# The sine product of the exchanged key halves on GpSimd instead of VectorE

## The reference, cut to what matters

```
x_attn = _L0_xattn_ref(_layernorm(x), ctx_4096, ctx_4096, mask, wq, wk, wv, wo, 0)

k = (key @ wk).reshape(bs, sk, N_KV_HEADS, 1, D_K)
rotate_half(x) = concatenate([-x2, x1])          # x1, x2: the halves of the 128
k = k * cos[None, None] + rotate_half(k) * sin[None, None]
raw = einsum('bhqd,bhkd->bhqk', q, k) / sqrt(D_K)
attn = softmax(raw + mask)
out = einsum('bhqk,bhkd->bhqd', attn, v)
```

## Time and profile before

| what | value |
|---|---|
| runs | 1937.64, 1943.05, 1941.91 us; median 1941.91 |
| the profiled execution | 1944.6 us, its span 1942.7 us |
| mean granted clock of TensorE | 0.984 |
| busy: TensorE, VectorE, ScalarE, GpSimd | 96%, 80%, 52%, 61% of the span |

### The profile page before, as it was taken

The page is one execution under the profiler, slowest core; times in us unless marked ns, Lnnn a source line. Parts: engine busy times, 40 slices in busy tenths (PEclk is TensorE's granted clock), DMA queues, the critical chain, the costliest instruction groups (busy, mean ns, idle before and its releaser), DMA issues. The chain is left out here.

```text
span 1942.7 us, 36348 instructions
## 1 busy us (share of the span) xinstructions
PE 1863.1 (96%) x12454; PEld 1706.5 (88%) x12454; DVE 1552.9 (80%) x2598; ACT 1019.1 (52%) x1882; POOL 1194.0 (61%) x990
## 2 busy tenths in 40 slices
PE   7989999999999999999999999999999999999688
PEld 7979998999889998999899988999899988999576
DVE  6768888888878888888888888888788888888244
ACT  5645555555555555555655555555455555556232
POOL 5627666666666674777566666776576656777300
PEclk9999999999999999999999999999999999999788
DMA  6622111112111111221112211111121110211270
GB/s 221 251 73 37 36 21 32 26 37 31 31 32 34 32 16 33 37 36 21 31 26 36 31 23 30 32 35 20 31 32 31 30 33 13 56 16 21 60 249 20
DMA packets 75303, 91.98 MB, mean 47 GB/s; under 512 B 22948, under 2 KB 49828, under 8 KB 75144
## 3 DMA queue, kind: packets, MB, share of 16 engines
q1 hardware_dynamic: 74136, 83.44, 20.2%
q10 hardware_dynamic: 1008, 6.42, 0.8%
HBM read 74.07 MB, written 15.77 MB: 46 GB/s over the span
## 5 line engine op out<-in xcount | busy, mean ns | idle before, releaser
L699 POOL TENSOR_TENSOR pT<-prob,pT 125x448 fp32r<-125x448 f32 x384 | 483.8, 1271 | 86.1 <-ACT pT L824 86.1
L881 PE MATMUL low_banks<-wv_hi,cT_hi 128*125 128x256 f32 x1536 | 434.4, 283 | 0.0
L881 PE MATMUL low_banks<-wv_hi,cT_lo 128*125 128x256 f32 x1536 | 432.7, 282 | 0.0
L881 PE MATMUL low_banks<-wv_lo,cT_hi 128*125 128x256 f32 x1536 | 432.3, 281 | 0.0
L765 ACT ACTIVATE k_work<-low_banks 64x500 f32<-64x500 f32 x384 | 223.8, 583 | 193.3 <-PE low_banks L865 186.1
L1081 DVE TENSOR_TENSOR prob<-t_banks,mask_t 125x448 f32<-125x448 f32 x384 | 235.3, 618 | 110.2 <-PE t_banks L916 95.4
L693 POOL TENSOR_TENSOR k_lo<-k_work,k_hi 128x500 fp32r<-128x500 f32 x192 | 253.8, 1322 | 110.1 <-ACT k_hi L773 110.1
L865 PE MATMUL low_banks<-cT_hi,wk_hi 128*128 128x500 f32 x768 | 315.5, 411 | 0.4 <-DVE cT_lo L1052 0.4
L710 POOL TENSOR_TENSOR sums<-sums,prob 125x448 f32<-125x448 f32 x252 | 291.0, 1155 | 26.8 <-ACT prob L818 25.8
L865 PE MATMUL low_banks<-cT_lo,wk_hi 128*128 128x500 f32 x768 | 298.8, 389 | 0.0
L865 PE MATMUL low_banks<-cT_hi,wk_lo 128*128 128x500 f32 x768 | 298.5, 389 | 0.0
(11 more groups left out here) (152 smaller groups left out, 3857.0 us busy)
## 6 DMA issues: line engine op xcount, KB each, us to landing
stage<-in_ctx_dram SPq DMA_DIRECT2D x72, 250.0 KB
inv_b<-inv_by_head SPq DMA_DIRECT2D x65, 112.0 KB, 4.8
attn_by_head<-attn SPq DMA_DIRECT2D x65, 112.0 KB, 1.7
wq_raw<-in_L_xattn_wq_dram SPq DMA_DIRECT2D x7, 1024.0 KB, 6.8
q_raw<-q_by_head SPq DMA_DIRECT2D x64, 112.0 KB, 4.9
head_rows<-in_ctx_dram SPq DMA_DIRECT2D x24, 250.0 KB
stage<-in_L_xattn_wo_dram SPq DMA_DIRECT2D x4, 1024.0 KB, 6.9
k_work<-in_L_xattn_wo_dram SPq DMA_DIRECT2D x4, 1024.0 KB, 7.7
```

The source lines that it names most:

```text
L699: nc.gpsimd.tensor_tensor(pT[:, j % PT_SLOTS, :, 1, :], pair(j), f32(pT[:, j % PT_SLOTS, :, 0, :]), ALU.subtract).then_inc(p_lo, 1)
L881: mm = nc.tensor.matmul(v_banks[0:ST, m % 2, t * PAIR:(t + 1) * PAIR], cT[a][:, d, tile * ST:(tile + 1) * ST], w[1][mv][:, d, g * DH:g * D ...
```

## The change

The sine product moves from VectorE's tables to GpSimd's, in every step and in the opening. The instruction is the same multiplication of the same operands, in place in `k_swap`; it still waits for the two copies of the exchange, and the rotation still waits for it. GpSimd's part waits once for the tables.

```
-    "even": ("comb qlow mred sub0 sub1 sub2 sin0 cos0 rot0 yred sin1 sub3 cos1 sub4 rot1 vlow3 sub5 mask0 sin2 "
+    "even": ("comb qlow mred sub0 sub1 sub2 cos0 rot0 yred sub3 cos1 sub4 rot1 vlow3 sub5 mask0 "
...
-    "even": "sum1 lo0 lo1 sum2 klow0 sum3 klow1 lo2 lo3 sum4 klow2 lo4 lo5 sum5 fin",
-    "odd": "sum1 lo0 klow0 lo1 sum2 lo2 klow1 lo3 klow2 sum3 lo4 sum4 lo5 sum5 fin",
...
+    "even": "sum1 lo0 sin0 lo1 sum2 klow0 sum3 sin1 lo2 klow1 lo3 sum4 sin2 lo4 klow2 lo5 sum5 fin",
+    "odd": "sum1 sin0 lo0 klow0 lo1 sin1 sum2 klow1 lo2 sin2 lo3 klow2 sum3 lo4 sum4 lo5 sum5 fin",
+    "turn": "lo0 lo1 sum1 sum2 sin0 sum3 lo2 klow0 sin1 sum4 lo3 klow1 sin2 lo4 lo5 klow2 sum5 fin",
+    "first": "sin0 klow0 sin1 klow1 sin2 klow2",
...
+        def k_sine(item, s, c):
+
+            pool.wait_ge(k_swapped, item * 2 + 2)
+            nc.gpsimd.tensor_tensor(k_swap[:, s], k_swap[:, s], tables[:, 1, c * SC:(c + 1) * SC], ALU.mult).then_inc(k_sined, 1)
...
+        pool.wait_ge(shared.tables_loaded, 32)
         pool.wait_ge(shared.q_stored[1], 16 * (HKV // 2 + 1))
...
+                if what == "sin":
+                    k_sine(k_item(b, g + 1, n), ((g + 1) * NC + n) % 2, n)
...
-        def k_sin_part(item, s, c):
-            dve.wait_ge(k_swapped, item * 2 + 2)
-            nc.vector.tensor_tensor(k_swap[:, s], k_swap[:, s], tables[:, 1, c * SC:(c + 1) * SC],
-                                    ALU.mult).then_inc(k_sined, 1)
```

More of the change, by code:

```diff
@@ L718, in _ @@
         for what, (n, *_) in tasks(POOL_STEP["first"]):
+            if what == "sin":
+                k_sine(n, n % 2, n)
             if what == "klow":
@@ L1121, in _ @@
                 k_cos_part(n, n % 2, n)
-            if what == "sin":
-                k_sin_part(n, n % 2, n)
             if what == "rot":
@@ L1163, in step @@
                     k_cos_part(kn + n, s, n)
-                if what == "sin":
-                    k_sin_part(kn + n, s, n)
                 if what == "rot":
```

## The result

The changed kernel takes 2350.45 us, the kernel before 1942.08 in the same session: ratio 1.211, 95% interval 1.207 to 1.215. I had forecast 2223, in a range of 2080 to 2290: the direction holds, the size does not.

What follows compares the result with a forecast made beforehand. TensorE was taken to bound even and odd steps. Even steps 150, odd steps 100, opening 4, turns -3 and clock 30 gave 281 us; 1944.6 + 281 - 2.7 = 2223, range 2080 to 2290.

Steps and rivals of the forecast that it cites:

- even steps, waits: Score fill 4 waits for the third key low part: 4.7 us in each of 32 even steps, first wait included.
- odd steps, waits: Score fill 2 waits for the bank emptied by mask addition 0, behind the third rotation: 4.15 us per odd step.
- clock in these steps: Gap ahead of score fill 4 brings half clock in half of 32 even steps, 1.84 us each: 30, bounds 0 and 59.
- opening: First sine waits on GpSimd for the query store, delaying rotation and context low part: 4 us, bounds 0 and 6.
- turns: Rotations stay where they were; late mask addition hides behind mask transposes, about 0.5 us gained in each of seven: -3.
- What bounds the kernel: TensorE is busy throughout even and odd steps; a lighter VectorE buys nothing, each added wait lengthens the run fully.
- Even step, first wait: Third key chunk waits for the bank freed by the rotation, which waits for the first sine: 1.3 us lost.
- Even step, last wait: Third key low part stands behind low part 4, which waits for high part 4: score fill 4 4.7 us later.
- The queue alone: First rival: no added waits between ScalarE and GpSimd, only GpSimd's queue length counts: 2053 us, chance 0.14.
- The dearer sine: Second rival: a sine on GpSimd takes 1.70 us instead of 1.22, 81 us more: 2304, chance 0.07.
- Not slower: Third rival: sines done in GpSimd's idle 6.69 us ahead of the first sum, collisions gone: about 1935, chance 0.04.

Runs made afterwards that it cites:

- the swap on GpSimd: Changed kernel with the third key low part ahead of low part 4 in GpSimd's order of even steps: 2178.8 us, ratio 1.124.
- the earlier places: Changed kernel with all sines still on GpSimd, only GpSimd's order in even and odd steps changed: 1948.2 us, ratio 1.006 to the kernel before.
- the move on VectorE: Changed kernel with mask additions 0 and 1 ahead of the third rotation in VectorE's order of odd steps: 2268.2 us, ratio 1.170.
- The filled gaps: Changed kernel plus 28 extra matmuls ahead of score fill 4 in even steps: 2256.0 us; with fillers in the odd steps' two gaps too: 2251.0 us.
- the kernel with the third sine alone: Only the third sine of each step on GpSimd, at its place in the changed kernel, the first two on VectorE: 2159.7 us, ratio 1.116.
- the kernel with the moved mask additions: Changed kernel with mask additions 0 and 1 ahead of the third rotation on VectorE in odd steps: 2268.2 us, ratio 1.170.

## Why the prediction was right and where it was wrong

| term | forecast | measured |
|---|---|---|
| even steps, waits | 32 x 4.7 = 150 | 32 x 5.73 = 183 |
| odd steps, waits | 24 x 4.15 = 100 | 24 x 4.29 = 103 |
| clock in these steps | 30 | 237.8 + 165.8 - 183 - 103 = 117 |
| opening | 4 | 5.2 |
| turns | -3 | 9.6 |
| the rest of the span | 0 | -5.6 |
| sum | 281 | 412 |

*What bounds the kernel.* Right: in even and odd steps TensorE had no wait to lose, and each added wait came out in full.

*Even step, first wait.* Right: the third key chunk starts 7.65 us after the step's start, walked 7.6.

*Even step, last wait.* The mechanism is right, shown by the swap on GpSimd that took this wait for high part 4 off the path. Its size was 1.0 short: 0.65 of it is there when the third sine ends (19.75 after the step's start, walked 19.1), the rest comes behind it. The walk took undisturbed durations, and GpSimd still met VectorE: the fourth sum took 1.53 beside the maximum of 1.50, the key low part 1.47; and low part 3 waited 0.55, not 0.4. In the mean of the 32 even steps these two take 1.52 and 1.47, with the earlier places 1.16 and 1.28. The rule of the Trainium skill (SBUF — State Buffer, "Who interferes with whom"), that a VectorE instruction with two SBUF inputs contends with a GpSimd instruction that reads SBUF, I had set aside as speaking for the change; the 1.53 beside the 1.50 agrees with it, and it worked against the change here. What the collisions cost in time is read from rows only: the run in which these two were short took the waits away as well.

*Odd step.* Right within 0.15, and the move on VectorE shows that the bank behind the rotation was the cause. That the third weighing would wait 0.75 ahead of it, on low part 2, the prediction did not have.

*Clock: the step that failed.* "I let half of the 32 cost it": all even steps lost 1.68 or thereabouts, and the odd steps, to which I gave nothing, lost up to 2.89 each, the dearer ones. I had priced the half clock by the one gap of each turn and looked for a single long gap; in an odd step two shorter ones (0.75 and 1.63) with one weighing between them did it, in 23 of the 24. The term came to 117 where I had 30: that is 87 of the 131 us that are missing, and the waits of the even steps are 33 more. The filled gaps show that this term is a cost of its own.

*Turns.* I had them 3 us shorter and had named a change of more than 2 us in them as a sign of being wrong; the median turn went from 36.07 to 39.15. Three of the seven took 36.4. The other four, among them the one shown, have a mean clock of 0.96, and in front of a context transpose a gap of 3.41, where the gaps before were 2.22 to 2.77. In the one shown VectorE's scaled output ahead of it had waited 4.25 us for the transfer of the inverse sums; why the gap is longer in these four stays open.

*Rivals.* The queue alone (2053) fell: the waits between ScalarE and GpSimd are there, 2.45 us to the forecast 2.4. The dearer sine fell: 1263 ns in the mean (the line below), my 1.26. Not slower did not happen, and its condition, a sine done ahead of the first sum, is what the earlier places made true: then 1948, not the 1935 that I gave it.

```profile
L699 POOL TENSOR_TENSOR k_work<-k_work,k_tables 128x500 f32<-128x500 f32 x192 | 242.5, 1263 | 18.3 <-ACT k_work L775 18.3
```

## What to carry to other kernels

Work that moves to an idle engine should be placed by when its data come and when its result is waited for, and then each instruction behind which the waiting engine's queue stands should be walked through; the idle share of an engine says nothing on this. When TensorE is bound, price a new wait twice: once as the gap, once as the slower matmuls after it, and count neighbouring gaps together. Before moving work, ask whether the engine relieved is waited for at all: here the seven turns' wait was worth 0.8%, and one instruction's place settled it.

## What the runs showed of the hardware that was not expected

- The length of a gap did not decide alone whether the clock fell. Two gaps of TensorE of 0.75 and 1.63 us, 0.89 apart, were followed by a stretch with a mean clock of 0.78; the same pair left one odd step of the changed kernel at 1.00 throughout (the first line below), and 17 of 24 odd steps of the kernel with the swap (0.80 and 1.62). A turn's single gap of 2.22 left the clock up before; in the kernel with the swap it fell in all four turns with a gap of 2.22 or 2.23 (the second line is one of them). Gaps of 2.8 in front of score fill 4 were followed by a fall in 14 of 32 even steps of the kernel with the third sine alone. What decides stays open.

```profile
1626.39:1656.37 29.98, 26.39 (x176) 23.84 (x175) 18.54 (x34) 13.54 (x26) 20.68 (x18) 1.00 0.12 13
349.73:387.63 37.90, 35.28 (x232) 31.78 (x231) 27.51 (x47) 20.48 (x38) 20.76 (x18) 0.95 0.17 40
```

- Removing the half clock of one kind of step moved that of the other, both ways: that of the odd steps went down when the even steps' gap was filled or shortened, that of the even steps went up when the odd steps' gaps were shortened. Why stays open.
- The two executions of the kernel with the moved mask additions took the same time, 2268.6 and 2267.9 us, at mean granted clocks of 0.943 and 0.898: over a whole span the mean clock gives no price. Why they differ stays open.
- TensorE idling can cost more than useless work: 896 added matmuls shortened the run by 94 us.
